# A diffusion-style block on one core: branch scales ahead of the second norm's scales, and a router softmax in two parts

## The reference

```
h = layernorm(x) * (1 + ca) + sa
h -> attention block: q = h Wq, feat = elu(q) + 1, linear attention with 8 heads -> msg (after Wm)
     h + layernorm(msg) + layernorm(relu(msg W1) W2)          # two branches, each with its own norm
x = x + ga * (that)
h = layernorm(x) * (1 + cb) + sb
logits = h Wg; probs = softmax(logits over 8 experts)
each expert takes its 512 most probable tokens; a token goes to one expert; out = weight * (gelu(h W1[e]) W2[e])
x = x + gb * out
```

## Time and profile before

| what | us |
|---|---|
| median of three runs | 280.78 (280.15 to 281.31) |
| the profiled execution | 277.45 |
| its span, first to last instruction | 275.70 |
| busy: TensorE, its weight loads, VectorE, ScalarE, GpSimd | 188.1, 147.9, 177.9, 124.2, 129.9 |

### The profile page before, as it was taken

How to read it: one execution, slowest core, us unless ns; L and a number is a source line. 1 busy time by engine, 2 the same in 40 slices (tenths; PEclk the granted TensorE clock), 3 DMA queues, 4 the chain that set the end, 5 groups by cost and what they waited for, 6 DMA issues and landing times.

```text
span 275.7 us, 4416 instructions
## 1 busy us (share of the span) xinstructions
PE 188.1 (68%) x1151; PEld 147.9 (54%) x1151; DVE 177.9 (65%) x660; ACT 124.2 (45%) x392; POOL 129.9 (47%) x207
## 2 busy tenths in 40 slices
PE   0788989796997797676758697751004995966740
PEld 0546759575776577671526275541004984856640
DVE  2779979999977666948898889900001895433340
ACT  2159964465597777435777642311001342232210
POOL 8737303142555445511995000777771037545572
PEclk9999999999799799555575999997555899899895
DMA  5892000001000000000567100434331334443310
GB/s 156 217 322 69 2 1 2 0 0 39 2 0 1 2 0 1 0 2 0 152 179 210 32 4 0 136 116 132 99 110 51 102 88 139 130 117 115 117 39 29
DMA packets 22009, 20.09 MB, mean 73 GB/s; under 512 B 2464, under 2 KB 19360, under 8 KB 21984
## 3 DMA queue, kind: packets, MB, share of 16 engines
q1 hardware_dynamic: 18752, 14.03, 17.2%
q0 software_dynamic: 2240, 5.51, 6.6%
q10 hardware_dynamic: 992, 0.27, 0.8%
HBM read 13.51 MB, written 6.29 MB: 72 GB/s over the span
## 4 chain that ended last, share of the span: by engine, by line
DVE 36%; PE 31%; another core or an unknown queue 11%; POOL 9%; issue 7%; ACT 4%; POOLq 1%; DVEq 0%
PE pQ L938 7%; PE pH L929 6%; DVE scr L1241 6%; DVE x_sb L1122 5%; DVE bn L977 2%; DVE t L1074 2%; POOL out_dram L402 2%; POOL yr L275 2%; PE pQ L648 2%; PE pH L755 2%; POOL rs L275 2%; DVE x_sb L1075 2%; DVE rows L985 2%; PE pQ L842 1%
## 5 line engine op out<-in xcount | busy, mean ns | idle before, releaser
L402 POOL DMA_INDIRECT out_dram<-rows,gidx x28 | 28.4, 1015 | 34.6 <-DVE rows L1389 28.2
L938 PE MATMUL pQ<-ew,u 128*128 (+1 forms) x140 | 25.6, 311 | 27.7 <-DVE dig L1413 21.0
L399 POOL DMA_INDIRECT rows<-table_dram,gidx x28 | 27.7, 988 | 31.5 <-DVE gidx L1333 23.3
L614 ACT ACTIVATE u<-pH 128x256 f32<-128x256 f32 x35 | 13.5, 386 | 58.5 <-remote 27.4
L938 PEld LDWEIGHTS pQ<-ew,u 128*128 128x128 f32 x140 | 21.4, 218 | 30.2 <-issue 28.3
L929 PE MATMUL pH<-x_sb,hid 128*128 (+1 forms) x140 | 25.7, 313 | 9.1 <-issue 7.9
L1381 DVE SCALAR_TENSOR_TENSOR t<-pQ,wslot,scr 128x128 f32<-128x128 f32 x35 | 12.3, 351 | 26.7 <-PE pQ L938 19.4
L929 PEld LDWEIGHTS pH<-x_sb,hid 128*128 128x128 f32 x140 | 21.5, 220 | 10.8 <-issue 10.7
L349 POOL TENSOR_TENSOR scr<-feat,z 128x512 f32<-128x512 f32 x8 | 9.6, 1202 | 23.0 <-DVE z L1101 23.0
L1365 DVE COPY inv<-pL 128x105 f32<-128x105 f32 x1 | 0.3, 269 | 30.4 <-remote 30.4
L755 PE MATMUL pH<-qT,mall 128*128 128x512 f32 x32 | 17.8, 686 | 0.0
(11 more groups left out here) (316 smaller groups left out, 526.9 us busy)
## 6 DMA issues: line engine op xcount, KB each, us to landing
hid<-in_L_ffn_W_dram SPq DMA_DIRECT2D x35, 128.0 KB
table_dram<-x_sb SPq DMA_DIRECT2D x9, 256.0 KB, 2.8
x_sb<-in_L_attn_x_dram SPq DMA_DIRECT2D x8, 256.0 KB, 7.5
table_dram<-rows SPq DMA_DIRECT2D x7, 256.0 KB, 2.3
ew<-in_L_ffn_W_dram SPq DMA_DIRECT2D x2, 512.0 KB, 8.5
w1d<-in_L_ffn_W_dram SPq DMA_DIRECT2D x1, 1024.0 KB, 9.8
rows<-table_dram,gidx POOLq DMA_INDIRECT x28
out_dram<-rows,gidx POOLq DMA_INDIRECT x28
```

What stands on the lines that cost most here:

```text
L399: gp.indirect_dma_start(row[:, t, :], None, table[:, :], bass.IndirectOffsetOnAxis(gidx[:, t:t + 1], 0)).then_inc(gathered[t], 16)
L402: gp.indirect_dma_start(out.rearrange("b l d -> (b l) d"), bass.IndirectOffsetOnAxis(gidx[:, t:t + 1], 0), row[:, t, D:2 * D], None).then_ ...
L614: act.activation(eh[:, i % 2, :], pH[i % 2][:, 0:F], ACT.Gelu).then_inc(S["eh_done"], 1)
L938: mm = te.matmul(pQ[i % 2][:, 0:D], eh[:, i % 2, f * P:(f + 1) * P], ew[:, bass.ds(e, 1), f * D:(f + 1) * D], start=(f == 0), stop=(f == 1))
```

## The change

On GpSimd, yrs(s-3) now stands ahead of rs3(s-4) in every step, as it did in the last two. Two waits ahead of the gathers change places.

The softmax is done in two parts. Part 0 takes the 24 tiles of groups 0 to 5, part 1 the 8 tiles of groups 6 and 7. VectorE's maximum and differences of part 0 are put into v_last, between the row nm of the last group and the normalising of its last two tiles; its sums, reciprocals and products behind these, ahead of the last h2. Part 1 stands where the softmax stood. ScalarE's exponential is made in two parts around a_h2_first. TensorE transposes both halves of group 7 ahead of the logits of group 6, waits for part 0's differences before it writes more logits, and transposes the probabilities per batch element (p_prt): the first ahead of the first up-projection, the second behind it. The keys are made per batch element too, the first between the differences and the sums of part 1. The banks of the two halves of group 7 are exchanged (pF for the first, pT for the second).

```diff
+SOFT = (((0, slice(0, TB)), (1, slice(0, TB - 2 * GT))), ((1, slice(TB - 2 * GT, TB)),))
+SOFT_TILES = ((0, NT - 2 * GT), (NT - 2 * GT, NT))
...
             for s in range(G + 6):
                 if s < G:
                     qprime(s)
-                if s == G + 2:
-                    yrs(G - 1)
-                if s == G + 1:
-                    yrs(G - 2)
+                if 0 <= s - 3 < G:
+                    yrs(s - 3)
                 if 0 <= s - 4 < G - 1:
                     rs3(s - 4)
                 if s - 4 == G - 1:
                     rs3_half(0)
                     rs3_half(1)
-                if 0 <= s - 3 < G - 2:
-                    yrs(s - 3)
...
+            gp.wait_ge(S["tab_done"], 16 * 2 * G)
             gp.wait_ge(S["slots_done"], 1)
-            gp.wait_ge(S["tab_done"], 16 * 2 * G)
...
+            def a_soft(part):
+                act.wait_ge(S["lmax"], part + 1)
+                for b, ts in SOFT[part]:
+                    last = act.activation(pe_[:, b, :, ts], m1[:, b, :, ts], ACT.Exp)
+                last.then_inc(S["exp2"], 1)
+
+            a_soft(0)
             a_h2_first()
+            a_soft(1)
...
             p_tx3_half(0)
+            p_tx3_half(1)
+            te.wait_ge(S["lmax"], 1)
             p_lg(G - 2)
-            p_tx3_half(1)
             p_lg_half(0)
             p_lg_half(1).then_inc(S["lg_ready"], 1)
...
+            def p_prt(b):
+                te.wait_ge(S["probs"], b + 1)
+                te.transpose(pT[:, b * P:(b + 1) * P], pr[:, b, :, :].rearrange("p e t -> p (e t)"), ident[:, :])\
+                  .then_inc(S["prt_ready"], 1)
+
+            p_prt(0)
             d_up(0)
...
+            p_prt(1)
             d_up(1)
...
+            def v_soft_max(part):
+                t0, t1 = SOFT_TILES[part]
+                dve.wait_ge(S["lg_ready"], (G - 2, G)[part])
+                link(dve.tensor_reduce(mxt[:, t0:t1], pL[:, t0 * E:t1 * E].rearrange("p (t e) -> p t e", e=E), AX.X, ALU.max))
+                lg = pL[:, 0:NT * E].rearrange("p (b t e) -> p b e t", b=B, e=E)
+                for b, ts in SOFT[part]:
+                    width = ts.stop - ts.start
+                    last = dve.tensor_tensor(m1[:, b, :, ts], lg[:, b, :, ts], mx[:, b, ts].unsqueeze(1).to_broadcast([P, E, width]),
+                                             ALU.subtract)
+                last.then_inc(S["lmax"], 1)
+
+            def v_soft_sum(part):
+                t0, t1 = SOFT_TILES[part]
+                dve.wait_ge(S["exp2"], part + 1)
+                for b, ts in SOFT[part]:
+                    last = dve.tensor_reduce(sm[:, b, ts], pe_[:, b, :, ts].rearrange("p e t -> p t e"), AX.X, ALU.add)
+                link(last)
+                link(dve.reciprocal(smt[:, t0:t1], smt[:, t0:t1]))
...
+            def v_key(b):
+                cs = slice(b * P, (b + 1) * P)
+                dve.wait_ge(S["prt_ready"], b + 1)
+                link(dve.tensor_scalar(ki[:, 0, cs], pT[:, cs].bitcast(I32), ((1 << 30) - 1) & -LOW, None, ALU.bitwise_and))
+                return dve.tensor_copy(khi[:, cs], ki[:, 0, cs])
...
                 dve.wait_ge(S["rs3"], G)
                 dve.scalar_tensor_tensor(nm[:, g, 0:2], mv[:, g, 0:2, 0], -1.0, rs[:, g, 0:2], ALU.mult, ALU.mult).then_inc(S["nm_done"], 1)
+                v_soft_max(0)
                 dve.wait_ge(S["rs3"], G + 1)
...
                 last.then_inc(S["xn3_last"], 1)
+                v_soft_sum(0)
                 dve.wait_ge(S["tx3"], G + 1)
...
+            v_soft_max(1)
+            v_key(0)
+            v_soft_sum(1)
+            dve.wait_ge(S["probs"], 2)
             dve.tensor_scalar(flat(prc), flat(pr), 2.0 ** -100, None, ALU.max)
...
+            v_key(1).then_inc(S["keys"], 1)
```

More of the change, by code:

```diff
@@ L529, in a_h2_first @@
                 act.wait_ge(S["lg_ready"], G - 2)
-                act.activation(h2T[:, (G - 1) % 2, 0:2 * P], pT[:, 0:2 * P], ACT.Identity, bias=colm[:, 2, B - 1:B],
+                act.activation(h2T[:, (G - 1) % 2, 0:2 * P], pF[:, 0:2 * P], ACT.Identity, bias=colm[:, 2, B - 1:B],
                                scale=colm[:, 3, B - 1:B]).then_inc(S["h2_done"], 1)
@@ L552, in _ @@
                     a_square(s - 3, 1, "y2_ready", "sq2")
+            def a_soft(part):
[4 more added lines that the diff above has]
+            a_soft(0)
             a_h2_first()
-            act.wait_ge(S["lmax"], 1)
-            act.activation(pe_[:, :, :, :].rearrange("p b e t -> p (b e t)"), m1[:, :, :, :].rearrange("p b e t -> p (b e t)"),
-                           ACT.Exp).then_inc(S["exp2"], 1)
+            a_soft(1)
             def d_gelu(k):
@@ L787, in p_tx3_half @@
                     te.wait_ge(S["xn3"], G)
-                    te.wait_ge(S["h2_done"], G - 1)
                 else:
                     te.wait_ge(S["xn3_last"], 1)
+                    te.wait_ge(S["h2_done"], G - 1)
                 for t in range(2 * h, 2 * h + 2):
-                    mm = te.transpose((pT, pF)[h][:, t * P:(t + 1) * P], xn[:, G - 1, t, :], ident[:, :])
+                    mm = te.transpose((pF, pT)[h][:, t * P:(t + 1) * P], xn[:, G - 1, t, :], ident[:, :])
                 mm.then_inc(S["tx3"], 1)
@@ L1148, in v_x1_half @@
                 last.then_inc(S["stats3"], 1)
+            mxt = mx[:, :, :].rearrange("p b t -> p (b t)")
+            smt = sm[:, :, :].rearrange("p b t -> p (b t)")
+            def v_soft_max(part):
[15 more added lines that the diff above has]
+                link(dve.reciprocal(smt[:, t0:t1], smt[:, t0:t1]))
+                for b, ts in SOFT[part]:
+                    width = ts.stop - ts.start
+                    last = dve.tensor_tensor(pr[:, b, :, ts], pe_[:, b, :, ts], sm[:, b, ts].unsqueeze(1).to_broadcast([P, E, width]),
+                                             ALU.mult)
+                last.then_inc(S["probs"], 1)
+            def v_key(b):
[3 more added lines that the diff above has]
+                return dve.tensor_copy(khi[:, cs], ki[:, 0, cs])
             def v_last():
@@ L1162, in v_last @@
                 last.then_inc(S["xn3_last"], 1)
+                v_soft_sum(0)
                 dve.wait_ge(S["tx3"], G + 1)
                 dve.wait_ge(S["lg_ready"], G - 2)
-                dve.tensor_scalar(h2T[:, g % 2, 2 * P:], pF[:, 2 * P:], colm[:, 3, B - 1:B], colm[:, 2, B - 1:B], ALU.mult, ALU.add)\
+                dve.tensor_scalar(h2T[:, g % 2, 2 * P:], pT[:, 2 * P:], colm[:, 3, B - 1:B], colm[:, 2, B - 1:B], ALU.mult, ALU.add)\
                    .then_inc(S["h2_last"], 1)
@@ L1211, in _ @@
             link(dve.tensor_copy(pH1[:, 0:2 * ROUNDS * NC], jst[:, :, :, :].rearrange("p k r c -> p (k r c)")))
[L1212 to L1225, removed]
+            v_soft_max(1)
+            v_key(0)
+            v_soft_sum(1)
+            dve.wait_ge(S["probs"], 2)
             dve.tensor_scalar(flat(prc), flat(pr), 2.0 ** -100, None, ALU.max)
-            dve.wait_ge(S["prt_ready"], 1)
             bits = pT[:, 0:B * P].bitcast(I32)
-            link(dve.tensor_scalar(ki[:, 0, :], bits, ((1 << 30) - 1) & -LOW, None, ALU.bitwise_and))
-            dve.wait_ge(S["consts"], 3)
-            dve.tensor_copy(khi[:, :], ki[:, 0, :]).then_inc(S["keys"], 1)
+            v_key(1).then_inc(S["keys"], 1)
             dve.wait_ge(S["keys"], 1)
```

## The result

| | before | after |
|---|---|---|
| median of four runs, us | 281.04 (280.15 to 281.52) | 285.51 (284.45 to 288.69) |
| profiled execution, us (span) | 277.45 (275.7) | 285.67 (283.9) |

The ratio of the runs is 1.023, 95% interval 1.017 to 1.029. The forecast was 282.3 in a range of 277.9 to 285.2: the change is slower, as forecast, but the median is 3.2 above the forecast, 0.3 outside the range. Part of the 3.2 is not the change: with its fourth run the old kernel's median is 281.04, 0.26 above the one that the forecast started from.

A forecast was written before the change was run, and what follows sets the result against it. The prediction took a second-phase loop of 7.88 us a step, replaced by a closed squares' loop of 8.49, as the bound. Loop +4.5 and tail -2.9 gave +1.6: 279.0 profiled, 282.3 us as median, range 277.9 to 285.2.

The forecast's parts named there:

- The loop is closed by the reorder: Second phase: squares, yr, rs, nm and normalising form a closed loop from the first step, 8.49 us a step against 7.88.
- The sum of the loop, +4.5 for x1(6): Second phase: four more loops of 8.49 bring x1(6) to 114.2 against 109.71, 4.5 us late.
- The tail, -2.9: Last norm to first search pass: split softmax starts the search at 126.55 against 129.48, 2.9 us gained, bounds 1.1 to 3.6.
- TensorE does not enter this phase: Second phase: TensorE ends y2 before ScalarE asks for it, leaving about 2.5 us that hides one short half-clock stretch.
- What follows is moved as a block: Search, slots, gathers and experts start from what the changed stretch delivers and only shift with it.
- The base: +3.3 from the profiled execution to the median: Whole kernel: the median, 280.78, lies 3.3 above the profiled 277.45; this difference was added to 279.0, giving 282.3.

The follow-up runs named there:

- e7: Changed kernel with GpSimd's q' of steps 4 to 7 waiting for the x1 of that step; ratio 0.997 to the old kernel.
- e1: Old kernel with only GpSimd's new order (yr of group g+1 ahead of rs of group g), softmax unsplit; ratio 1.022 to the old kernel.
- e3: Changed kernel with ScalarE's normalising xn3 put behind the y2 squares of the same step; ratio 1.009 to the old kernel.
- e4: Old kernel with four more unused squares of y1 on ScalarE in each second-phase step; one run, 282.75 us against 279.19.
- e6: Changed kernel with GpSimd's old order put back and q' of steps 4 to 7 waiting for x1; ratio 0.972 to the old kernel.
- c0: Old kernel unchanged, profiled a second time on one of the faster chips (also written c0_before); 251.57 us, one run.
- e6b: Same kernel as e6 (split softmax, GpSimd's old order, late q'), run again on another chip; 274.61 us, ratio 0.976 to the old kernel.
- e8: Split softmax and late q' as in e6, with rs ahead of yr for group 6 too; 275.07 us, ratio 0.978 to the old kernel.
- e9: Old kernel with only q' of steps 4 to 7 put behind x1; ratio 0.990 to the old kernel.
- a0_after: Changed kernel unchanged, run again on one of the faster chips; ratio 1.011 to the old kernel.

## Why the prediction was right and wrong, step by step

- **The loop is closed by the reorder: right.** It starts at the step forecast, x1(1) to x1(2), ends at group 6, and has the pieces named. Its plain period is 8.34 where I had 8.49: from the start of the normalising to the end of the next y2 squares it takes 86.15-81.48 = 4.67, where I had 4.82.
- **The sum of the loop, +4.5 for x1(6): mis-sized, 5.5 measured.** The term that failed is the 3.67 from the end of the y2 squares to the start of xn3: it took 90.67-86.15 = 4.52 in two of the steps. I had it from group 6, where no q' runs, and wrote of q' only as what slows x1 in the old order. But under the new order the q' of the two steps at 80 and 89 us starts right behind rs, beside nm, and nm is inside the loop, ahead of both the normalising and x1: 1.01-0.16 = 0.85, twice, 1.7. Without these 1.7 the phase would have grown by 3.8, less than forecast, since the plain period is shorter too; e7 has +3.1, 0.8 of the difference being its first gap. The row to read was the second x1 of the earlier trace rows beside that of the earlier trace rows: 1.92 against 1.14 for the same instruction was already there, and the question to ask was what q' would lie beside once moved.
- **The tail, -2.9: right, -2.99**, and by its steps: the last h2 is 11.52 behind x1(6) in place of 12.77 (1.25 earlier; 1.13 forecast), and the search 5.27 behind it in place of 7.00 (1.73; 1.8 forecast). The 64-column maximum, difference and product take 0.22 each and the sum 0.26, where I took 0.2, and the reciprocal of 8 columns 0.20. The split adds eight VectorE instructions and not seven (part 0's sum takes two); the sum of the tail didn't rest on that count.
- **TensorE does not enter this phase: right** for the changed kernel's order (e1's step above); e3, e4 and e6 show where it does.
- **"What follows is moved as a block": wrong by 1.07.** Behind the search TensorE's up-projections stand ahead of the threshold's transpose. After:
```profile
158.34 2.06 PE L836 MATMUL pQ<-h2T,w1d 128*128 128x512 f32 x2
...
160.26 0.58 PE L880 MATMUL pG<-ident,thi 128*128 128x8 f32 x2
```
Before:
```profile
155.42 1.10 PE L832 MATMUL pQ<-h2T,w1d 128*128 128x512 f32 x2
...
156.47 0.39 PE L873 MATMUL pG<-ident,thi 128*128 128x8 f32 x2
```
  The same work meets half clock after and full clock before (the 23rd digit of the clock's line is 5 above and 9 in the earlier trace rows). The stretch is 0.83 in before, c0, e6b, e8 and e9 and 1.44 to 1.90 in the other nine profiles, so it is where the work falls against the clock's changes, not a step of the change. I had not asked what a shift of some us does to that.
- **The base: +3.3 from the profiled execution to the median: not settled.** The stretch from indices to weights took 38.42 in the profiled old kernel and 40.6 to 41.4 in the six other profiles on chips of its kind, so the profiled difference, 8.2, probably overstates the change by some 2.5. The old kernel has no second profile on such a chip that would show it. How the medians' 4.5 divide isn't shown either: +5.5 and -3.0 make 2.5, and the profiles' +1.1 and +0.4 would make it 4.0. Where the gathers don't stall, the medians of a0_after and the old kernel are 2.4 apart (256.0 and 253.61), which would be phase and tail alone; but the profiled executions there, 256.50 and 251.57, are 4.9 apart and have the +1.1 too.

The failed step is therefore the size of the loop's term, 1.0 too small, because q' stretches nm inside the loop. The threshold's 1.07, which the profiled execution has on top, may be part of the rest; with it about two thirds of the 3.2 missed would be found. What else lies behind the threshold isn't settled.

## What to carry to other kernels

When an operation is moved ahead of another on an in-order engine, write down all that stands behind the delayed one on every other engine, up to what feeds the moved one; if that closes a circle whose sum is above the old period, it is the new period, and an earlier result for one step buys nothing. Then ask of each instruction in that circle what will run beside it in the new order: durations carry over from the old trace only with the same neighbour. And try the two halves of a change apart: here one was worth 3 us, the other cost 5.6, and where it cost pointed to a further change, the delay of one GpSimd instruction that takes 3.6 off the same phase.

## What the runs showed of the chip

- **One GpSimd product stretches a small VectorE instruction sixfold.** nm, 4 columns: 0.16 alone, 1.01 beside q' (after, a0_after, e3); x1's first four: 1.13 and 1.92; the statistics 0.87 both ways (e7).
- **Two kinds of chips.** The old kernel takes 279 to 282 us on some and 253.6 on two others, with the same instructions. The difference lies in indices to weights, 38.4 to 41.4 against 11.2; the old kernel's two profiles, one of each kind, agree within 1.3 us in every other stretch. On both kinds GpSimd is issuing its 28 gathers then. VectorE of the changed kernel:
```profile
217.12 0.27 DVE L1394 COPY inv<-pL 128x105 f32<-128x105 f32 x1 [33.27 <-remote]
```
  It waits for TensorE's signal behind these matmuls, which the trace has long before:
```profile
192.31 1.21 PE L954 MATMUL pL<-featT 128*128 128x105 bf16 x14
```
  In c0_before, the old kernel on one of the others, VectorE:
```profile
182.75 0.27 DVE L1365 COPY inv<-pL 128x105 f32<-128x105 f32 x1 [3.22 <-PE pL L947]
```
  There the copy follows its matmuls (181.85, 0.86) at once; on the other chips it comes more than 20 us after them, and the trace names nothing on this core that released it. No experiment was made on the cause, and it stays open.
